# Q of two batches side by side in fp32r, and the shared expert's weights loaded late

## What is computed

```
def xattn(x, ctx, Wq, Wk, Wv, Wo, bo):        # x 16x112x256, ctx 16x375x256, 16 heads of 64
    q = layernorm(x) @ Wq                      # 256 -> 1024
    k = ctx @ Wk; v = ctx @ Wv                 # 256 -> 1024 each
    attn = softmax(q_h @ k_h.T / 8)            # per batch and head, 112x375
    return concat_h(attn_h @ v_h) @ Wo + bo
x = x + xattn(...)
x = x + expert_of_token(layernorm(x)) + (relu(layernorm(x) @ sw1 + sb1) @ sw2 + sb2)   # shared expert: sw1, sw2
...
```

## Time and profile before

| | us |
|---|---|
| median of 3 runs | 957.97 (956.17 to 958.02) |
| profiled execution | 958.77 |
| its span | 956.0 |
| granted TensorE clock, mean of the span | 0.981 |

### The profile page before, as it was taken

One profiled execution on the slowest core, in us unless ns is written; L12 is line 12 of the kernel. 1 busy time (PEld: TensorE's weight loads), 2 busy tenths in 40 slices (PEclk: granted clock), 3 DMA queues, 4 the chain that ended last, 5 costly groups with the idle time before them and its releaser, 6 DMA issues.

```text
span 956.0 us, 19821 instructions
## 1 busy us (share of the span) xinstructions
PE 903.7 (95%) x6730; PEld 794.5 (83%) x6730; DVE 623.0 (65%) x1634; ACT 525.6 (55%) x1258; POOL 268.2 (28%) x337
## 2 busy tenths in 40 slices
PE   5889999999999999999999999998989999998864
PEld 4779888898888988889898898887878999996643
DVE  6766666767667676676766767665654666348777
ACT  4655565555655556555565555654742555446633
POOL 1323333333333333333433334333100000041214
PEclk9999999999999999999999999999999999999985
DMA  9230000000000000000000000000550142265502
GB/s 290 97 106 17 2 18 5 21 16 5 16 5 21 16 5 16 5 21 16 5 16 5 21 14 7 0 5 9 162 190 20 54 169 85 63 193 163 155 6 77
DMA packets 29459, 50.56 MB, mean 53 GB/s; under 512 B 2480, under 2 KB 24080, under 8 KB 27648
## 3 DMA queue, kind: packets, MB, share of 16 engines
q1 hardware_dynamic: 27888, 46.42, 15.6%
q0 software_dynamic: 1536, 3.67, 1.3%
HBM read 41.83 MB, written 8.26 MB: 52 GB/s over the span
## 4 chain that ended last, share of the span: by engine, by line
PE 88%; DVE 7%; ACT 2%; issue 2%; DMA 1%; POOL 0%; DVEq 0%
PE bank L1648 27%; PE bank L1677 10%; PE bank L1841 9%; PE bank L1696 9%; PE bank L1861 8%; PE bank L1662 8%; PE bank L1630 6%; PE bank L1717 5%; PE bank L1950 2%; PE bank L1968 1%; DVE norm_stats L1023 1%; PE bank L1811 1%; PE bank L1609 1%; PE bank L1957 1%; DMA x_all<-in_x 1%
## 5 line engine op out<-in xcount | busy, mean ns | idle before, releaser
L664 POOL TENSOR_TENSOR probs<-probs,row_rcp 112x375 f32<-112x375 f32 x256 | 202.4, 813 | 415.8 <-DVE row_rcp L1118 415.3
L784 ACT ACTIVATE probs<-bank,neg_max 112x375 f32<-112x375 f32 x256 | 144.4, 570 | 69.0 <-DVE neg_max L1112 68.9
L1677 PE MATMUL bank<-ident,probs 112*125 112x112 f32 x768 | 129.1, 277 | 2.3 <-DVE probs_t L1123 2.3
L1677 PEld LDWEIGHTS bank<-ident,probs 112*125 112x125 f32 x768 | 113.8, 187 | 18.2 <-issue 3.3
L1112 DVE TENSOR_REDUCE neg_max<-bank 112x1 f32<-112x375 f32 x256 | 123.3, 539 | 7.6 <-PE bank L1662 7.5
L1123 DVE COPY probs_t<-bank 125x336 f32<-125x336 f32 x128 | 64.7, 506 | 70.1 <-PE bank L1677 66.8
L756 ACT ACTIVATE k_parts<-bank 128x376 fp32r<-128x376 f32 x128 | 62.1, 485 | 69.3 <-PE bank L1648 69.3
L1648 PE MATMUL bank<-ctx_hi,wk_hi 128*128 128x376 f32 x256 | 97.2, 380 | 2.3 <-DVE k_parts L1103 1.5
L759 ACT ACTIVATE v<-bank 125x512 f32<-125x512 f32 x96 | 57.4, 598 | 57.2 <-PE bank L1648 57.1
L1696 PE MATMUL bank<-probs_t,v 125*64 125x112 f32 x1536 | 87.7, 263 | 0.6 <-ACT probs_t L772 0.6
L1696 PEld LDWEIGHTS bank<-probs_t,v 125*64 125x64 f32 x1536 | 74.0, 137 | 16.9 <-issue 16.7
(11 more groups left out here) (208 smaller groups left out, 1877.0 us busy)
## 6 DMA issues: line engine op xcount, KB each, us to landing
stage<-in_ffn_up SPq DMA_DIRECT2D x6, 1024.0 KB, 5.4
stage<-in_ffn_down SPq DMA_DIRECT2D x6, 1024.0 KB, 7.5
ctx_raw<-in_ctx_t SPq DMA_DIRECT2D x16, 375.0 KB, 3.4
ring_late<-in_ctx_t SPq DMA_DIRECT2D x10, 375.0 KB, 6.8
ring_late<-in_ctx_n SPq DMA_DIRECT2D x10, 375.0 KB
routed<-xn SPq DMA_DIRECT2D x1, 2240.0 KB, 11.1
rows_in<-routed SPq DMA_DIRECT2D x5, 448.0 KB, 6.1
answers<-y_rows SPq DMA_DIRECT2D x10, 224.0 KB, 2.7
```

Of the source, the lines that this page charges most:

```text
L664: eng.tensor_tensor(probs[s][:, :], probs[s][:, :], row_rcp[:, s:s + 1].broadcast_to([S, C]), ALU.mult).then_inc(probs_ready, 1)
L784: eng.activation(probs[r][:, :], SCORE_BANKS[i][0:S, 0:C], ACT.Exp, bias=neg_max[:, r:r + 1], accum_out=row_sum[:, r:r + 1]).then_inc(exp_ ...
L1677: t = eng.transpose(turn_bank(i, project)[0:CJ, j * S:(j + 1) * S], probs[QUAD * v + i][:, j * CJ:(j + 1) * CJ], ident[0:S, 0:S])
```

## The change

**Q of two batches at once.** From batch 2 on, the normalised tokens of an even batch and of the odd one after it are kept side by side as `xq_hi` and `xq_lo` (2 x 112 = 224 columns), and Wq as `wq_hi`, `wq_lo`. A half's Q of both batches comes from two units, PAIR_UNIT (-1, bank 1) and Q_UNIT (0, bank 0), each 12 fp32r products of 224 columns. So the half before an even batch's half computes nine units (called *heavy* here), the half before an odd batch's half seven (*light*, no Q). Heavy halves are the c=1 halves of odd batches 1 to 13 and the c=0 halves of even batches 2 to 14, light ones the c=1 halves of even batches and the c=0 halves of odd batches from 2 on: 14 each. The four halves of Q of batches 0 and 1 stay as they were, fp32 and each for itself. 28 units of 8 fp32 products go, 28 of 12 fp32r products come.

**Steps.** The units are given to the eight places of a half by a table: heavy [-1] [0] [1] [2] | [3] [4] [5] [6, 7], light [1] [2] [3] [4] | [5] [6] [7] [].

**Tokens.** The copy of the transposed tokens goes to `xq_hi` on ACT (`pair_out` for `tokens_out`), and their rest is a new operation on DVE, `pair_rest`, in c=1 v=0 after the first two maxima, from batch 1 on.

**Weights late.** Wq's split parts lie in the memory of the shared expert's up weights, Wk's in that of the down weights. The expert's raw pieces go through `wq_sb` once Wq is split: the up piece is loaded in batch 1 and split at the end of batch 14 (c=1 v=1); the down piece is loaded after the loop and split in the last batch in c=1 v=0, where the first `split_shared` now stands too. In batch 0 Wq is split in the place of the up piece (c=0 v=1), nothing in that of the down piece (c=1 v=1).

**The loop** now runs over pairs of batches (6 turns).

The core of the diff:

```
+                return {1: [[k] for k in range(8)],
+                        2: [[PAIR_UNIT], [Q_UNIT], [1], [2], [3], [4], [5], [6, 7]],
+                        0: [[1], [2], [3], [4], [5], [6], [7], []]}[self.queries]
@@ PE, unit @@
+                if k <= Q_UNIT and f.queries == 2:
+                    if k == PAIR_UNIT and cf == 0:
+                        eng.wait_ge(xq_split, bf)
+                    for i in range(2):
+                        col = (PAIRS * cf + 2 * (k - PAIR_UNIT) + i) * P
+                        n = 0
+                        for kt in range(KT):
+                            w = [t[:, kt, col:col + P] for t in (wq_hi, wq_lo)]
+                            a = [t[:, kt, :] for t in (xq_hi, xq_lo)]
+                            for wp, ap in split_products((w, a)):
+                                m = eng.matmul(bank[k % 2][:, 2 * i * S:2 * (i + 1) * S], wp, ap, start=(n == 0),
+                                               stop=(n == 3 * KT - 1))
+                                n += 1
@@ DVE, in each visit @@
                         largest_scores(visit, v, 0)
+                        if v == 0 and rest is not None:
+                            pair_rest(rest, rest % 2 if isinstance(rest, int) else odd)
...
-                            unit_lo(u + 1, QUAD * v, 1 - c)
+                        step_rest(0)
                         pair_rcp(visit, v, 2)
...
                             norm2_steps(b - 1, 7 * v, 7 * v + 4)
-                        if project and v == 0:
-                            unit_lo(u + 1, 1, 1 - c)
+                        step_rest(1)
                         if v == 1 and not first:
                             heads_rest(u - 1)
...
-                        if first and v == 1:
-                            piece_lo(FFN_PIECE + c)
+                        step_rest(3)
+                        if isinstance(b, int) and b == B - 2 and c == 1 and v == 1:
+                            piece_lo(FFN_PIECE)
-                        if last and c == 0 and v == 1:
-                            eng.wait_ge(proj_ready[0], unit_count(u + 1, 4))
+                        if last and c == 1 and v == 0:
+                            eng.wait_ge(proj_ready[1], units.all(1))
                             split_shared(0)
+                            piece_lo(FFN_PIECE + 1)
@@ SP @@
-            load_piece(FFN_PIECE)
-            load_piece(FFN_PIECE + 1)
             batch(0)
...
+            load_piece(FFN_PIECE)
+            with eng.Fori(2, B - 2) as b:
                 batch(b)
+            load_piece(FFN_PIECE + 1)
```

323 lines of the change are left out of this document (212 added, 111 removed).

## The result

The changed kernel takes 985.55 us (median of 4 runs, 985.01 to 986.56) where the kernel before takes 957.40 beside it: a ratio of 1.0305, 95% interval 1.0288 to 1.0323. The forecast was 985 with a range of 967 to 993. Its profiled execution has a span of 984.8 us, 28.8 more than before.

A forecast was written before the change was run, and what follows sets the result against it. PE bounds the kernel, busy 95% of the span with 88% of the chain of waits. Q's -11.2 us, added waits and the opening's -1.0 sum to +27.0: 985.8 in the profile, median 985 us, range 967 to 993.

The forecast's parts named there:

- the clock: Last batch: PE runs at a slower clock once after a wait, put at 1.5 us.
- Q's products: In the loop: a group of 12 fp32r products costs 1.46 us instead of 1.86; over 28 places, -11.2 us.
- V6's wait: Odd batches, c=1 v=1: K4's rest, behind the norm's chain, reaches PE at 9.25; V6 waits 1.9; +12.3 us.
- Even batches, c=1: v=1: project_out waits 1.3 us instead of .2, +7.7; v=0: K1 waits for ctx_lo, +4.3, and T1, +1.2.
- c=0: Heavy halves have K4's rest ready; light ones bring project_out forward, about .3 us late, seven times: +2.1 us.
- 81.5 to 82 us: Loop: a pair of batches takes 81.5 to 82 us where two batches take 80.
- The hold: c=1 v=1: DVE's norm_term of 112x1 numbers takes 2.68 us, beginning beside POOL's multiplications and ending with them.
- The last batch: Batches 14 and 15, late splits: T1 waits 3.0 us, the last visit's chain +5.0, slower clock 1.5; +9.5 in all.
- The opening: Opening: without the down piece's split, all of it moves up by about a microsecond: -1.0 us, up to -2.6.
- A: Rival: the fp32r product of 224 columns runs at the fp32 rate, +100 us on top, about 1085; chance 6%.
- B: Rival: norm_term falls before POOL's three multiplications, V6 doesn't wait; sum -1.8 us, at the best end 955 to 957; 8%.
- C: Rival: waits overlap, small ones don't occur beside big ones, or Q costs .102 a product; 969 to 974 us; 16%.

The follow-up runs named there:

- the two runs on POOL: Changed kernel with the indirect DMA of c=1 moved from v=1 to v=0, 970.64 us; the same plus an ordinary POOL operation in the DMA's old place, 972.58 us.
- the run with the heads first: Changed kernel with K4's rest and heads_lo both ahead of the norm's chain on DVE in c=1 v=1: 966.88 us, ratio 1.0083.
- the best version with pairs: Changed kernel, K4's and heads' rests first, indirect DMA in v=0, odd batches' statistics and ctx_lo behind first copy, late splits in c=0 v=1: 957.99 us, ratio 0.9992.

## Why the prediction was right, and where it wasn't

It named the mechanism, the places and nearly the sum: +27.0 on the profile, measured +28.8. That the total is so near is in part luck: the clock was under-priced by 5.4 us, and four other differences took back most of that. Point by point:

- **Q's products**: predicted 1.46 us a group, measured 1.42, at .111 a product. -12.3 instead of -11.2. As forecast, 224 columns cost what 112 of fp32 cost (.112), so the columns don't set this time; that the weight load sets it fits, but no run changed the weights alone. The Trainium skill's 107 ns a load of 128 columns ("TensorE: Matmul & The Clock Gate", section "LDWEIGHTS (loading the stationary operand)") lies 4% under the .111 measured; the value taken from the neighbouring row, .117, 5% over it.
- **V6's wait**: start at 9.25 predicted and measured, to the hundredth. Its price, by the visit without it, is 1.96, predicted 1.9. The visit is 13.85, where the prediction's terms give 13.95 (11.11 + 1.11 + 1.93 - .2). Only batch 1 had clearly less, 12.51 against 11.89 without the wait, .6 instead of .9. **v=0** there: T1 waits .29, not .5, but the visit is 9.32, and the terms give 9.35.
- **Even batches, c=1**: `project_out` at 9.32 predicted and measured; the moved K place is lost to the last tenth, 11.10 against 11.11. v=0 is 9.12, predicted 9.00 (8.90 - .75 + .65 + .2).
- **c=0**: odd batches 8.14 and 10.12, predicted 8.15 and 10.19; even ones 8.76 and 12.05, predicted 8.85 and 12.11. All four halves together: 82.46 a pair of batches, where the prediction's terms add up to 82.7. Its own sign, "81.5 to 82 us", doesn't fit its terms and was missed. The mean busy share of PE in the loop is .96, as it said (about .95).
- **The hold** was explained wrongly, and the sum didn't feel it. The row of 2.68 us was read as the multiplications'; it takes the indirect DMA ahead of them, as the two runs on POOL show. An operation that meets the multiplications alone loses at most the rest of one (.81). That agrees with the rule of the Trainium skill that I weighed ("SBUF — State Buffer", section "Who interferes with whom": the loser blocks for the other's instruction), and not with my reading of it, which let it block for several.
- **The last batch** was priced right for a partly wrong reason. T1 waited 2.46 (predicted 3.0), and the maxima of the last visit came 4.6 later (predicted 4.9). But the subtraction there wasn't held until 3.12 us of multiplications had ended, as the prediction had it from its reading of the hold. It waited for one multiplication, the next multiplication waited for it, and so on in turns: 1.58 and 3.58 us on DVE and 5.33 on POOL by the rows of the last batch. That is again the block for one instruction. The wait of 4.43 came before T2 and T3, not before T0 as its sign said.
- **The clock** is the term that was mis-sized. The prediction put 1.5 us in one place. The rows show four: 1.54 in batch 3 and in batch 9, 1.6 behind the up piece (12.40 against the 10.84 of the run with the heads first, with the same wait of 2.46), and by estimate 2.3 in the last visit, 6.9 us in all. Against that stand 1.6 us that the six pairs of batches came out shorter, .2 in batch 1, about 1.3 of shorter waits in the last batch, and 1.1 in the expert part, which was to have the same length. The opening brought .6 and not 1.0 (.1 up to batch 1's first scores, .5 in its first visit, where PE waits 1.96 instead of 2.57). So the sum is nearer than its terms: with the low clock where the prediction had it, the time would have been about 980.
- **Rivals.** A (fp32 rate) fell with the .111. B (the hold doesn't reach K4's rest) is what the run with the DMA in v=0 made true on purpose: it came out at 970.64, not at B's 955 to 957. The six pairs of batches 2 to 13 are 2.6 us longer there than before, where B's sum has them 6.9 shorter: Q brought 12.3, not 16.1 (3.3 of the difference in these pairs), V6's visits were still .66 us longer than without a wait (4.0 in all), and of the waits in the halves with seven units, which B dropped, some .23 stayed in each (2.8). C didn't occur: the small waits stood beside the big ones in every visit.

Where did Q's 12.3 us go, once the orders were mended? By the visits of the best version with pairs: 1.0 us a pair of batches to K1 and T1 in even c=1 v=0, where Q no longer stands ahead of K1 (9.11 against the 8.14 of odd c=0, with the same four K places and no wait), .4 to the tokens in even c=1 v=1, .3 in odd ones. Q's products, fp32 and slow, had covered the context's split. That part is argued from visit lengths; no run filled the place with other work.

## What to carry to other kernels

Cheaper work on the bounding engine is worth only what the other engines can follow; look at the start time that each consumer wants after the change, and at what each of its operands stands behind, in program order, on its producer. A long operation with an odd length (2.68 us for 112 numbers) is a hazard wherever a consumer stands behind it: put what others wait for ahead of it, which was worth 0.3 to 0.4% here even without any other change. And an idle stretch of the matrix engine can cost more than its length: behind 6 of the 18 waits of 1.71 us, and all 13 of 3.07, slower products came on top. The prediction counted them once and was 5.4 us short by it.

## What the runs showed of the hardware

- A DVE operation with two operands in SBUF, 112x1 each, takes .15 us alone, up to .81 while POOL multiplies 112x375, and 2.68 when POOL has issued an indirect DMA just ahead of three such multiplications; an ordinary operation in the DMA's place gives .51, .73 and .74 for one DVE operation each.
- Two rows of long operations, one on each engine, take turns, one operation at a time: in the last batch a multiplication ends about .67 us after DVE's operation, and a rest of 128x1024 1.08 after the multiplication. In the rows both look stretched: 1.09 becomes 1.58, 2.36 becomes 3.58, and four multiplications of 3.12 become 5.33.
- Behind an indirect DMA of POOL a 112x1 operation of DVE gets no turn between the multiplications: it is held for those left of the three (1.60, 2.21 and 2.68, by where it begins; in batch 2 for two of the three, 1.63).
- Products come slower, at a lower granted clock, behind some idle stretches of PE: behind none of .41 or .70 us in odd batches, behind 6 of the 18 of 1.71 (three kernels; batches 3 and 9 in two of them, 3 and 11 in the third), behind 4 of the 5 of 2.46 in batch 15, behind all 13 of 3.07. Where a visit with the same wait and the full clock stands beside it, it cost 1.5 to 1.6 us (15.39 against 13.85, 12.40 against 10.84). The same wait of 1.95 in the opening was followed by it in some profiles and not in others, so the length of the wait alone doesn't decide.
- An fp32r product of 224 columns comes every .111 us, of 256 columns every .117, with new 128-column weights for each.
